# Moving GpSimd's row scatters and value copies behind the weighted sums in a fused attention and mixture-of-experts kernel

## The chip, the cores and the metric

The program runs on one core of a Trainium2 chip. The metric is the time of one execution in microseconds (us), the median of three runs. The core's engines work side by side, each on its own list of instructions, and meet at semaphores: PE (TensorE, matrix multiplication; PEld is its loading of weights), ACT (ScalarE), DVE (VectorE), POOL (GpSimd) and SP (SyncE, which here only issues DMAs).

## The reference, cut to what matters

The input has 8 batches of 512 rows of 128 values. A layer of causal attention with 16 heads of 8 values is followed by a layer that sends every row to its 2 best of 8 experts:

```python
x = L0_attn_x                       # (8, 512, 128)
x = x + attention(layernorm(x))     # causal softmax, 16 heads of 8
# the second layer, on s * b = 4096 rows of 128
probs = jax.nn.softmax(x_flat @ gate_w.T)
topk_probs, topk_idx = jax.lax.top_k(probs, 2)
hidden = relu(einsum('th,ehf->tef', x_flat, w1) + b1)
all_out = einsum('tef,efh->teh', hidden, w2) + b2
y = sum(gathered_by(topk_idx) * topk_probs)
x = x + y
```

The kernel does not compute all experts for all rows. It sorts the rows by expert in memory and works on blocks of 128 rows of one expert.

## The kernel before, in words

**Two stages.** The attention stage is a loop over 8 batches `b` and, in each, 4 groups of 4 heads `g`: 32 steps `s = 4b + g`. The expert stage then works through blocks of 128 sorted rows. Nothing schedules the kernel: each engine has its own function `step(b, g, ...)`, and the order written there by hand is the order in which its instructions run. An engine that waits holds up everything behind it in its list.

**One attention step.** PE makes the scores of step `s + 2` (`scores`, line 998, in 11 pieces; `psS`), and DVE takes their row maxima (`maxima`, lines 1349 and 1352). PE makes the transposed, shifted scores of step `s` (`probs`, line 1011, 10 pieces numbered `n`; `psT`), and ACT takes their exponentials into `PT` (`exps`, line 811). Between them, early in step `s`, PE multiplies the exponentials of step `s - 1` by the values (`weigh`, line 1035, 32 matmuls into `psO`). Its last matmul raises `pv_done`. ACT waits for that to copy the sums out (`copy_heads`, line 816, `Os`), PE then turns them (`turn_heads`, line 1053), and DVE divides them (`norm`). Right behind its weighted sums PE also transposes the split maxima (line 1045, `psM`), and ACT copies those (line 823, `shiftT`).

**What POOL does in a step.** It zeroes the upper triangle of `PT` in four parts: `mask(s, 0)` once `exps(s, 3)` is done, `mask(s, 1)`, `mask(s, 3)`, `mask(s, 2)` once later exponentials are (line 598). It copies the values of a group that the weighted sums have finished with to `Vs` (`load_v`, line 586, four copies, after `pv_done`). In the first group it makes the third part of K (`third_k`, line 559). It splits the maxima of step `s + 2` into three parts (`split_shift`, lines 609 to 617). And it issues the row scatters.

**The row scatters.** A scatter (`scatter`, line 629) is one indirect DMA that POOL issues: 128 normalised rows of 130 values of `xn2` go to the places in `sorted_x` that `place` names. A batch has 4 tiles of 128 rows and 2 experts per row, so 8 scatters. Those of batch `b - 2` are issued in batch `b`, which needs that batch's `place` (semaphore `placed`, by DVE) and `xn2` (`xn2_ready`, by ACT). There are 64 in all, 48 of them in the attention stage from batch 2 on, two in most steps. One stands at a step's end, behind `split_shift`, and so runs into PE's next step; the other stands behind `load_v`. In the last batch there are up to three in a step.

**The counting step.** In the fourth group of a batch (the third group in the last batch) PE counts the rows of each expert for batch `b - 1`: `count_rows`, lines 1073 to 1079, 11 small matmuls in a row. The last one raises `ranks_ready`. DVE makes the places from that.

The program's own names `Qs`, `Ks`, `Vs`, `Os`, `PT`, `psS`, `psT`, `psO`, `psM` are buffers in SBUF or PSUM; `xn` in the rows stands for `xn2` as well.

Of the kernel before, what the change touches and what calls it, by code (L numbers as in the profile page):

```python
# [17 lines left out]
CH = T // P  # L18
TILES = BATCH * CH
GROUPS = 4  # L20
# [13 lines left out]
E, F, TOPK = 8, 512, 2  # L34
# [45 lines left out]
def late_batch(b):  # L80

    return int(b >= KNOWN)
# [50 lines left out]
def prob_turn(s, n):  # L133

    return (s * NPROB + n) % RING, (s * NPROB + n) // RING
# [7 lines left out]
def layer(nc, x, wq, wk, wv, wo, bo, gate_w, w1, b1, w2, b2, out):  # L143
    with ExitStack() as ctx:
# [6 lines left out]
        def sem(name):  # L151
            return ctx.enter_context(nc.semaphore(name))

        def sems(name, n):
            return [sem(f"{name}{i}") for i in range(n)]
# [138 lines left out]
        v_ready, v_copied = sem("v_ready"), sem("v_copied")  # L294
# [7 lines left out]
        prob_ready, prob_done, masked = sems("prob_ready", RING), sems("prob_done", RING), sem("masked")  # L302
        pv_first, pv_done = sem("pv_first"), sem("pv_done")
# [12 lines left out]
        picks_done, ranks_ready, ranks_kept, placed, routed, exp_done = (  # L316
            sem(n) for n in ("picks_done", "ranks_ready", "ranks_kept", "placed", "routed", "exp_done"))
# [192 lines left out]
        def _(pool):  # L510
            def own_wait():

                pool.sem_inc(pool_turn, 1)
# [41 lines left out]
            def third_k(b):  # L555
                u = b % 2
                pool.wait_ge(k_second, b + 1)
                own_wait()
                pool.tensor_tensor(kparts[:, u, 2, :], krest[:, u, :], kparts[:, u, 1, :], ALU.subtract).then_inc(ksplit_done, 1)

            def add_bias(b):
                pool.wait_ge(xn_ready, b + 1)
                own_wait()
                xs = x_all[:, b * CH:(b + 1) * CH, :]
                pool.tensor_tensor(xs, xs, bo_b[:, :].unsqueeze(1).to_broadcast([P, CH, D]), ALU.add).then_inc(xb_done, 1)
# [17 lines left out]
            def load_v(b, g):  # L583
                own_wait()
                for c in range(CH):
                    last = pool.tensor_copy(Vs[:, g, c, :, 0:HD],
                                            v_all[:, b * CH + c, g * 32:(g + 1) * 32].rearrange("p (h d) -> p h d", d=HD))
                last.then_inc(v_loaded, 1)
# [31 lines left out]
            def scatter(b, number):  # L620

                c, k = number // TOPK, number % TOPK
                pool.wait_ge(placed, b + 1)

                if b == BATCH - 2:
                    pool.wait_ge(xn2_last, c + 1)
                else:
                    pool.wait_ge(xn2_ready, (b if b < BATCH - 2 else b - 1) * CH + c + 1)
                pool.indirect_dma_start(  # L629
                    out=xs_dram, out_offset=bass.IndirectOffsetOnAxis(ap=place[:, b, k, c:c + 1], axis=0),  # L630
                    in_=xn2[:, b * CH + c, :], in_offset=None).then_inc(scattered[late_batch(b)], 16)

            def step(b, g, first, last):
                s = b * GROUPS + g
                if last and g > 0:
                    bank, turn = prob_turn(s, 2)
                    pool.wait_ge(prob_done[bank], turn + 1)
                    scatter(b - 2, 3 * g - 2)

                masks = not (last and g == GROUPS - 1)  # L640
                if masks:
                    mask(s, 0)
                if not (first and g == 0) and not (last and g > 0):

                    pool.wait_ge(pv_done, s)
                    pool.wait_ge(v_copied, b + (g + 3) // GROUPS + 1)
                    load_v(b + (g + 3) // GROUPS, (g + 3) % GROUPS)
                if g == 0 and AHEAD_QKV <= b + 1 < BATCH:
                    third_k(b + 1)


                if b >= 2 and g > 0 and not last:
                    scatter(b - 2, 2 * g - 1)
                if last and 0 < g < 3:
                    scatter(b - 2, 3 * g - 1)
                if b >= 3 and g == 0:
                    scatter(b - 3, CH * TOPK - 1)
                if masks:
                    mask(s, 1)
                    mask(s, 3)  # L660
                    mask(s, 2)
                if not (last and g >= 2):
                    split_shift(s + 2, (g + 2) % GROUPS)
                if g == 1 and b + AHEAD_QKV < BATCH:
                    add_bias(b + AHEAD_QKV)
                if g == 3 and b + AHEAD_QKV < BATCH:
                    score_x(b + AHEAD_QKV)
                if b >= 2 and not (last and g > 0):
                    scatter(b - 2, 2 * g)
                if last and 0 < g < 3:  # L670
                    scatter(b - 2, 3 * g)
                if last and g == 3:
                    scatter(b - 1, 0)

# [1202 lines left out]
```

## Time and profile before

| what | us |
|---|---|
| median of three runs | 506.52 |
| lowest and highest of the three | 505.99, 507.28 |
| span of the profiled execution | 527.7 |
| PE busy in that span | 469.7 |
| DVE busy | 413.1 |
| ACT busy | 358.9 |
| POOL busy | 286.6 |

The profiled execution is one run of the same program with the recording of every instruction switched on. Its span, from the first to the last instruction, is 21.2 us longer than the median of the runs without recording. A line of the timeline gives when an operation begins, how long it takes, its engine, line and tiles, how often it is repeated without a gap, and in brackets how long the engine was idle before it and whose work ended the idle time.

### The profile page before, as it was taken

How to read it: one execution, taken by the hardware profiler on the slowest of the kernel's cores; microseconds unless marked ns; L12 is line 12 of the kernel's file. 1: busy time of each engine (PE TensorE's matmuls, PEld its weight loads, DVE VectorE, ACT ScalarE, POOL GpSimd, SP SyncE). 2: the span in 40 equal slices, each digit the busy share in tenths (PEclk: the TensorE clock that was granted, in tenths of full speed). 3: DMA queues.
4: the chain of work that ended last, by engine and by line, in shares of the span. 5: the costliest groups of instructions: out<-in, count | busy, mean ns of one | idle time of the engine just before them, and what ended most of it. 6: DMA issues, size and time to landing. Idle time of an engine off the chain costs nothing.

```text
span 527.7 us, 14330 instructions
## 1 busy us (share of the span) xinstructions
PE 469.7 (89%) x4121; PEld 328.0 (62%) x4121; DVE 413.1 (78%) x1519; ACT 358.9 (68%) x782; POOL 286.6 (54%) x579
## 2 busy tenths in 40 slices
PE   3788999999999999999999999989788789999981
PEld 1545656556555545546555545459688679999980
DVE  6898878988988888888888897875556555557875
ACT  7576877777867867876866857875456457777750
POOL 5603544535755766657657565725456555545542
PEclk9879999999999999999999999999999899999997
DMA  7434232132233233233333326722222322235653
GB/s 225 134 93 129 56 118 91 56 118 88 67 120 108 70 108 110 76 101 97 102 95 98 106 76 175 209 65 63 56 63 69 85 77 74 71 79 180 182 172 101
DMA packets 49454, 54.92 MB, mean 104 GB/s; under 512 B 6564, under 2 KB 41554, under 8 KB 49377
## 3 DMA queue, kind: packets, MB, share of 16 engines
q1 hardware_dynamic: 44736, 45.18, 29.5%
q0 software_dynamic: 4320, 8.47, 4.7%
q8 instruction: 35, 0.57, 0.5%
q14 instruction: 43, 0.34, 0.2%
q10 hardware_dynamic: 320, 0.36, 0.2%
HBM read 34.96 MB, written 17.90 MB: 100 GB/s over the span
## 4 chain that ended last, share of the span: by engine, by line
PE 50%; DVE 28%; ACT 7%; issue 7%; DMA 4%; another core or an unknown queue 3%; ACTq 1%; SPq 0%; POOL 0%; DVEq 0%; POOLq 0%
PE psO L1035 12%; DVE psS L1349 10%; PE psT L1197 7%; DVE maxs L1352 7%; PE psS L998 7%; PE psM L1208 5%; PE psO L1208 5%; PE psT L1011 3%; PE psS L1197 2%; ACT PT L811 2%; DMA xs_t<-sorted_x 2%; PE psS L1187 2%; DVE maxs L1349 1%; DVE xn L1278 1%
## 5 line engine op out<-in xcount | busy, mean ns | idle before, releaser
L811 ACT ACTIVATE PT<-psT 128x512 f32<-128x512 f32 x320 | 172.5, 594 | 67.6 <-PE psO L1035 45.0
L1349 DVE CUSTOM_DVE_ANT_0 psS<-mask_row,psS 128x512 f32<-128x512 bf16 (+1 forms) x232 | 142.8, 624 | 33.6 <-PE psS L998 29.3
L998 PE MATMUL psS<-Ks,Qs 96*128 96x128 bf16 (+3 forms) x512 | 132.9, 308 | 9.5 <-DVE maxs L1352 7.3
L598 POOL TENSOR_SCALAR_AFFINE_SELECT PT<-PT 128x512 f32<-128x512 f32 x124 | 76.8, 635 | 96.0 <-ACT PT L811 94.8
L1011 PE MATMUL psT<-Qs,Ks 108*128 108x384 bf16 (+3 forms) x512 | 109.9, 299 | 4.2 <-ACT PT L811 3.0
L695 POOL DMA_INDIRECT token_y<-Qs,y_row x71 | 70.8, 997 | 74.6 <-DVE Qs L1750 39.0
L998 PEld LDWEIGHTS psS<-Ks,Qs 96*128 96x128 bf16 x512 | 50.4, 99 | 53.5 <-DVE maxs L1352 26.4
L629 POOL DMA_INDIRECT sorted_x<-xn,place x64 | 64.3, 1005 | 27.6 <-issue 16.5
L1352 DVE TENSOR_REDUCE maxs<-psS 128x2 f32<-128x512 f32 (+3 forms) x120 | 75.7, 669 | 1.8 <-PE psS L1001 1.4
L1035 PE MATMUL psO<-PT,Vs 128*32 128x512 f32 (+3 forms) x1024 | 75.8, 436 | 0.3 <-DVE x_all L1375 0.3
L1011 PEld LDWEIGHTS psT<-Qs,Ks 108*128 108x128 bf16 x512 | 43.5, 97 | 32.8 <-ACT PT L811 12.9
L1197 PE MATMUL psT<-turned,qrest 128*128 128x128 f32 x428 | 61.0, 280 | 1.3 <-ACT qrest L887 0.9
L895 ACT ACTIVATE krest<-psT,turned 128x128 f32<-128x128 f32 x142 | 44.7, 365 | 25.7 <-PE psT L1197 8.1
L1197 PEld LDWEIGHTS psT<-turned,qrest 128*128 128x128 f32 x428 | 54.1, 194 | 2.6 <-issue 2.5
L1035 PEld LDWEIGHTS psO<-PT,Vs 128*32 128x32 f32 x1024 | 28.6, 109 | 40.9 <-issue 27.4
L1001 PE MATMUL psS<-mask_row,identb 128*128 128x128 bf16 x280 | 49.9, 226 | 0.0
L887 ACT ACTIVATE qrest<-w_sb 128x512 f32 x71 | 44.6, 630 | 0.4 <-issue 0.4
L882 ACT ACTIVATE turned<-psS 128x128 f32<-128x128 f32 x71 | 19.7, 278 | 35.5 <-PE psS L1187 17.0
L1208 PE MATMUL psO<-w_sb,krest 128*128 x288 | 40.4, 285 | 3.4 <-ACT krest L895 2.3
L1208 PE MATMUL psM<-w_sb,krest 128*128 x280 | 38.2, 279 | 5.7 <-ACT krest L895 3.1
L1743 DVE TENSOR_SCALAR krest<-psS,turned 128x128 f32<-128x128 f32 x70 | 21.5, 347 | 23.0 <-PE psS L1197 12.1
L1208 PEld LDWEIGHTS psO<-w_sb,krest 128*128 128x128 f32 x288 | 36.6, 199 | 4.5 <-issue 4.4
(260 smaller groups left out, 741.1 us busy)
## 6 DMA issues: line engine op xcount, KB each, us to landing
Qs<-q_parts SPq DMA_DIRECT2D x96, 96.0 KB
Ks<-k_parts SPq DMA_DIRECT2D x95, 96.0 KB
xs_t<-sorted_x SPq DMA_DIRECT2D x71, 65.0 KB
w_sb<-in_L_ffn_w SPq DMA_DIRECT2D x16, 256.0 KB
k_parts<-kparts SPq DMA_DIRECT2D x8, 384.0 KB, 2.6
q_parts<-qparts SPq DMA_DIRECT2D x8, 384.0 KB, 3.6
x_all<-in_L_attn_x SPq DMA_DIRECT2D x8, 256.0 KB, 4.7
v_all<-token_y SPq DMA_DIRECT2D x4, 512.0 KB, 4.4
```

The costliest lines, as they stand in the source:

```text
L598: pool.affine_select(out=square, in_=square, compare_op=ALU.is_ge, fill=0.0, base=0, pattern=[[0, GH], [1, P]], channel_multiplier=-1).the ...
L629: pool.indirect_dma_start(out=xs_dram, out_offset=bass.IndirectOffsetOnAxis(ap=place[:, b, k, c:c + 1], axis=0), in_=xn2[:, b * CH + c, :] ...
L695: pool.indirect_dma_start(out=token_y, out_offset=bass.IndirectOffsetOnAxis(ap=y_row[:, i % (2 * Y_RING):i % (2 * Y_RING) + 1], axis=0), i ...
L811: act.activation(PT[:, n * T:(n + 1) * T], psT[:, bank, :], ACT.Exp).then_inc(prob_done[bank], 1)
L998: last = pe.matmul(psS[:, bank, c0:c0 + n], Qs[0:QK_ROWS, g, h, j * P:n], Ks[0:QK_ROWS, g, h, 0:n], start=True, stop=alone)
L1001: last = pe.matmul(psS[:, bank, c0 + n - P:c0 + n], identb[:, :], mask_qk[:, :], start=False, stop=True)
L1011: last = pe.matmul(psT[:, bank, c0:c0 + T - i * P], Ks[0:ST_ROWS, g, h, i * P:(i + 1) * P], Qs[0:ST_ROWS, g, h, i * P:T], start=True, stop ...
L1035: last = pe.matmul(psO[h * VW:(h + 1) * VW, i * P:T], Vs[:, g, i, h, :], PT[:, c0:c0 + cols], start=(i == KEY_BLOCKS[0]), stop=(i == KEY_B ...
L1197: last = pe.matmul(bank[:, c0:c0 + P], w1_t[:, i % 2, c * P:(c + 1) * P], xsT[:, i % 2, :], start=True, stop=True)
L1208: last = pe.matmul(ps_v[i % 2][:, 0:D], hT[:, i % 2, c * P:(c + 1) * P], w2_sb[:, bass.ds(e, 1), c, :].rearrange("p a d -> p (a d)"), star ...
L1349: dve.tensor_tensor_reduce(src, mask_row[:, (CH - 1 - j) * P:], src, 1.0, NEG, ALU.add, ALU.max, maxs[:, par, j, h:h + 1]).then_inc(scores ...
L1352: dve.tensor_reduce(maxs[:, par, j, h:h + heads], src, AX_X, ALU.max).then_inc(scores_used[bank], 1)
```

## The change

All of it is in POOL's list, and no instruction is added or taken away but waits. `load_v`, with its wait for `pv_done`, goes from behind `mask(s, 0)` to the step's beginning. The scatter that stood at a step's end goes to the next step, behind that wait and those copies, ahead of `mask(s, 0)`. The other scatter stays behind `mask(s, 0)`, where now no copies stand between the two; `third_k` goes ahead of it by the same copies. In the counting step it also waits for `ranks_ready`. In the last batch, where `load_v` is over, the wait for `pv_done` alone opens the step, and the waits for exponentials are placed one by one.

```diff
+            def weigh_over(s):
+                pool.wait_ge(pv_done, s)
+
+            def exps_over(s, n):
+                bank, turn = prob_turn(s, n)
+                pool.wait_ge(prob_done[bank], turn + 1)
...
             def step(b, g, first, last):
                 s = b * GROUPS + g
+                masks = not (last and g == GROUPS - 1)
+                if not (first and g == 0):
+                    weigh_over(s)
+                if not (first and g == 0) and not (last and g > 0):
+                    pool.wait_ge(v_copied, b + (g + 3) // GROUPS + 1)
+                    load_v(b + (g + 3) // GROUPS, (g + 3) % GROUPS)
+                if b >= 2 and g > 0:
+                    scatter(b - 2, 3 * (g - 1) if last else 2 * (g - 1))
+                if b >= 3 and g == 0:
+                    scatter(b - 3, CH * TOPK - 2)
+
                 if last and g > 0:
-                    bank, turn = prob_turn(s, 2)
-                    pool.wait_ge(prob_done[bank], turn + 1)
+                    exps_over(s, 2)
                     scatter(b - 2, 3 * g - 2)
-
-                masks = not (last and g == GROUPS - 1)
                 if masks:
                     mask(s, 0)
-                if not (first and g == 0) and not (last and g > 0):
-
-                    pool.wait_ge(pv_done, s)
-                    pool.wait_ge(v_copied, b + (g + 3) // GROUPS + 1)
-                    load_v(b + (g + 3) // GROUPS, (g + 3) % GROUPS)
                 if g == 0 and AHEAD_QKV <= b + 1 < BATCH:
                     third_k(b + 1)
-
-
+                if b >= 2 and g == (2 if last else 3):
+                    pool.wait_ge(ranks_ready, b)
                 if b >= 2 and g > 0 and not last:
                     scatter(b - 2, 2 * g - 1)
-                if last and 0 < g < 3:
-                    scatter(b - 2, 3 * g - 1)
                 if b >= 3 and g == 0:
                     scatter(b - 3, CH * TOPK - 1)
+                if last and 0 < g < 3:
+                    if g == 1:
+                        exps_over(s, 6)
+                    scatter(b - 2, 3 * g - 1)
+
                 if masks:
                     mask(s, 1)
                     mask(s, 3)
...
-                if b >= 2 and not (last and g > 0):
-                    scatter(b - 2, 2 * g)
-                if last and 0 < g < 3:
-                    scatter(b - 2, 3 * g)
                 if last and g == 3:
                     scatter(b - 1, 0)
```

POOL's list in batch 2, from the end of the second step (L565 adds a bias) into the third. Before:

```order
L565 TENSOR_TENSOR x_all<-x_all,bo_b 128x512 [waits xn_ready]
L629 DMA sorted_x<-xn,place 33920x130 [waits xn2_ready,placed]
L598 AFFINE_SELECT PT<-PT 128x4x128 [waits prob_done1]
L586 COPY Vs<-v_all 128x4x8 [waits pv_done,v_copied]
L586 COPY Vs<-v_all 128x4x8 x3
L629 DMA sorted_x<-xn,place 33920x130 [waits xn2_ready,placed]
```

The same place in the changed kernel:

```order
L565 TENSOR_TENSOR x_all<-x_all,bo_b 128x512 [waits xn_ready]
L586 COPY Vs<-v_all 128x4x8 [waits pv_done,v_copied]
L586 COPY Vs<-v_all 128x4x8 x3
L629 DMA sorted_x<-xn,place 33920x130 [waits xn2_ready,placed]
L598 AFFINE_SELECT PT<-PT 128x4x128 [waits prob_done1]
L629 DMA sorted_x<-xn,place 33920x130 [waits xn2_ready,placed]
```

The first scatter and the four value copies now follow PE's weighted sums, and the mask stands between the two scatters.

POOL's list in the fourth step of batch 2, the counting step, from the last part of `split_shift` (L617) of the step before it. Before:

```order
L617 TENSOR_TENSOR mparts<-mrest,mparts 128x4x4 [waits shift_step]
L629 DMA sorted_x<-xn,place 33920x130 [waits xn2_ready,placed]
L598 AFFINE_SELECT PT<-PT 128x4x128 [waits prob_done2]
L586 COPY Vs<-v_all 128x4x8 [waits pv_done,v_copied]
L586 COPY Vs<-v_all 128x4x8 x3
L629 DMA sorted_x<-xn,place 33920x130 [waits xn2_ready,placed]
L598 AFFINE_SELECT PT<-PT 128x4x128 [waits prob_done0] x2
```

The same place in the changed kernel:

```order
L617 TENSOR_TENSOR mparts<-mrest,mparts 128x4x4 [waits shift_step]
L586 COPY Vs<-v_all 128x4x8 [waits pv_done,v_copied]
L586 COPY Vs<-v_all 128x4x8 x3
L629 DMA sorted_x<-xn,place 33920x130 [waits xn2_ready,placed]
L598 AFFINE_SELECT PT<-PT 128x4x128 [waits prob_done2]
L629 DMA sorted_x<-xn,place 33920x130 [waits xn2_ready,placed,ranks_ready]
L598 AFFINE_SELECT PT<-PT 128x4x128 [waits prob_done0] x2
```

Here the second scatter also has a wait for PE's count, and the masks of later exponentials stand behind it. The lists of the other four engines are unchanged.

## Rows read from the trace of the kernel before

**Rows 1.** The page: the span, and busy time, share and instructions of each engine.
```profile
span 527.7 us, 14330 instructions
...
PE 469.7 (89%) x4121; PEld 328.0 (62%) x4121; DVE 413.1 (78%) x1519; ACT 358.9 (68%) x782; POOL 286.6 (54%) x579
```

**Rows 2.** Who waited for whom, whole span: total us, times, longest us.
```profile
ACT Os L816 <- PE psO L1035: 9.8, 13, 1.0
...
PEld psS L998 <- DVE maxs L1352: 26.4, 58, 0.9
```

**Rows 3.** Timeline of POOL, batch 4, second step: start us, us, operation, idle before.
```profile
208.59 1.00 POOL L629 DMA_INDIRECT sorted_x<-xn,place  x1 [0.49 <-issue]
212.78 0.63 POOL L598 TENSOR_SCALAR_AFFINE_SELECT PT<-PT 128x512 f32<-128x512 f32 x1 [3.19 <-ACT PT L811]
213.36 0.65 POOL L586 COPY Vs<-v_all 128x32 f32<-128x32 f32 x4
214.17 1.00 POOL L629 DMA_INDIRECT sorted_x<-xn,place  x1 [0.16 <-issue]
216.34 1.21 POOL L598 TENSOR_SCALAR_AFFINE_SELECT PT<-PT 128x512 f32<-128x512 f32 x2 [1.17 <-ACT PT L811]
```

**Rows 4.** Timeline of ACT: copies of the weighted sums (L816), one exponential (L811).
```profile
107.57 0.60 ACT L816 ACTIVATE Os<-psO 128x512 f32<-128x512 f32 x1
...
189.12 0.60 ACT L816 ACTIVATE Os<-psO 128x512 f32<-128x512 f32 x1 [0.49 <-PE psO L1035]
...
194.36 1.57 ACT L811 ACTIVATE PT<-psT 128x512 f32<-128x512 f32 x3 [0.24 <-PE psT L1011]
...
199.08 0.60 ACT L816 ACTIVATE Os<-psO 128x512 f32<-128x512 f32 x1
...
210.20 0.60 ACT L816 ACTIVATE Os<-psO 128x512 f32<-128x512 f32 x1 [0.92 <-PE psO L1035]
```

**Rows 5.** Timeline of PE: the 32 matmuls of weighted sums; steps of batches 1, 3, 4.
```profile
85.86 2.36 PE L1035 MATMUL psO<-PT,Vs 128*32 128x512 f32 x32
...
95.53 2.36 PE L1035 MATMUL psO<-PT,Vs 128*32 128x512 f32 x32
...
105.14 2.36 PE L1035 MATMUL psO<-PT,Vs 128*32 128x512 f32 x32
...
114.94 2.36 PE L1035 MATMUL psO<-PT,Vs 128*32 128x512 f32 x32
...
186.35 2.36 PE L1035 MATMUL psO<-PT,Vs 128*32 128x512 f32 x32
...
196.65 2.36 PE L1035 MATMUL psO<-PT,Vs 128*32 128x512 f32 x32
...
207.00 2.36 PE L1035 MATMUL psO<-PT,Vs 128*32 128x512 f32 x32
...
217.28 2.36 PE L1035 MATMUL psO<-PT,Vs 128*32 128x512 f32 x32
```

**Rows 6.** Timeline of PE: turning the copied sums, batches 1 and 4.
```profile
89.35 0.60 PE L1053 MATMUL psO<-identf,Os 128*128 128x128 f32 x4
...
210.85 0.66 PE L1053 MATMUL psO<-identf,Os 128*128 128x128 f32 x4 [0.20 <-ACT Os L816]
```

**Rows 7.** Timeline of DVE: two first maxima after the sums, and one square-root step.
```profile
108.07 0.70 DVE L1349 CUSTOM_DVE_ANT_0 psS<-mask_row,psS 128x512 f32<-128x512 bf16 x1 [1.00 <-PE psS L998]
...
189.90 0.70 DVE L1349 CUSTOM_DVE_ANT_0 psS<-mask_row,psS 128x512 f32<-128x512 bf16 x1 [1.64 <-PE psS L998]
...
202.76 0.89 DVE L1418 SCALAR_TENSOR_TENSOR rstd<-near,guess 128x4 f32<-128x4 f32 x1
```

**Rows 8.** One-microsecond stretches: length, busy us and count by engine, clock, DMA, GB/s.
```profile
199.10:200.10 1.00, 1.00 (x8) 0.55 (x6) 0.53 (x1) 1.00 (x3) 1.00 (x1) 1.00 0.42 147
...
208.60:209.60 1.00, 1.00 (x25) 0.67 (x18) 0.47 (x3) 0.68 (x2) 0.99 (x1) 1.00 0.36 111
...
213.40:214.40 1.00, 1.00 (x15) 0.74 (x12) 0.85 (x4) 1.00 (x4) 0.84 (x6) 1.00 0.00 1
```


## The prediction, made before the changed kernel was run

> **What bounds the kernel now.** I read the page first. In a span of 527.7 us PE is busy for 469.7 and DVE for 413.1, while POOL, the only engine whose list changes, is busy for 286.6 [rows 1]. POOL has time to spare, so the change can only matter through those who wait for POOL, or through what POOL's work does to its neighbours. The table of waits comes next. PE waits for DVE's maxima 58 times, 26.4 us in all, and ACT waits for the end of PE's weighted sums before it copies them, 13 times, 9.8 us in all, 0.75 us each [rows 2]. Then I read POOL's timeline in one step. The scatter at the step's end begins at 208.59 and lasts 1.00; the first mask comes at 212.78 after 3.19 us of idle time, then the value copies (0.65), the second scatter (1.00) and, after 1.17 us idle, the next masks [rows 3]. Between the two scatters POOL mostly waits for ACT.
>
> The thing to see is what stands beside the first scatter. In the second step of batch 4 the weighted sums begin at 207.00 and end at 209.36 [rows 5], in the middle of the scatter of 208.59 to 209.59 [rows 3]. ACT starts its copy at 210.20 [rows 4], 0.84 after that end. In the fourth step of batch 1, where no scatter exists yet, the sums end at 107.50 [rows 5] and the copy starts at 107.57 [rows 4]: 0.07. In the fourth step of batch 3 it is 189.12 against 188.71: 0.41. In the first step of batch 4 the sums end at 199.01 and the copy starts at 199.08, again 0.07, though POOL is in a scatter from then on [rows 4, 5, 8]. So PE's word that the sums are over reaches ACT late when it falls inside a scatter, and on time when it falls ahead of one. That is what the change is about: it puts the first scatter behind that word.
>
> **The change part by part.** *The first scatter leaves the end of the sums.* What the late word costs can be read in three places. PE turns the copied sums 1.13 after their end in batch 1 (89.35 against 88.22) and 1.49 after it in batch 4 (210.85 against 209.36) [rows 5, 6]: 0.36 lost on PE. DVE takes its first maximum behind the sums 0.57 after their end in batch 1 (108.07) and 1.19 after it in batch 3 (189.90 against 188.71) [rows 5, 7]: 0.62 lost on DVE. And whole fourth steps take 9.80 in batch 1 (105.14 to 114.94) and 10.30 in batch 3 (186.35 to 196.65): 0.50 [rows 5]. Second steps take 9.67 and 10.28 [rows 5], 0.61 apart, of which I give the scatter only PE's 0.36, since ACT has normalisations to do there from batch 2 on. Five second steps (batches 2 to 6) by 0.36 make 1.8, five fourth steps by 0.50 make 2.5, and the three waits that are left of the 13, in the last batch, by 0.36 make 1.1: together 5.4 us of the profiled span. The bounds are 0 and 13 by 0.62, or 8.1.
>
> *What the first scatter meets in its new place.* After the sums' end come the copies (0.65), a gap of 0.16 and the scatter (1.00) [rows 3]: about 1.8 us, with the signal some 2. The first mask starts at 212.78, 3.4 after the end of the sums. So it hides with 1.4 to spare, and POOL's idle time of 3.19 is the cover; if that were gone, each step would lose up to 1.8. I take 0.
>
> *The second scatter and the copies.* With the copies out of the way the second scatter starts 0.65 earlier, at some 213.5 instead of 214.17, and the masks behind it, which wait for ACT in any case (1.17 idle), lose nothing [rows 3]. The same goes for the third part of K in the first steps: 0.65 earlier on POOL, with nobody waiting. It can change what it blocks, though: in a first step an operation of DVE on 4 values per partition takes 0.89 [rows 7]. At most it frees or costs 0.65 in each of five steps, 3.3 either way. I take 0, since the maxima's waits of PE stand elsewhere in most steps.
>
> *The wait for the count.* Six counting steps now hold POOL until PE has counted. Behind the waiting scatter stand three masks and the splitting of the maxima, and PE waits for the latter. On PE's own list the count stands ahead of the scores' exponentials that the next mask needs, so POOL's 1.17 of idle time covers the scatter's 1.00 plus 0.16 [rows 3]: barely. The bounds are 0 and six by 1.16, or 7.0. I take 0, because the mask can't start before ACT's exponential, which comes later than the count. The gain there is bounded by ACT's wait of 0.24 at 194.36, just behind a count [rows 4], and is already in the 0.50.
>
> *The last batch.* The wait for an exponential ahead of the third scatter of the second step may push the masks back by a scatter, 1.0 us once at most; I take 0.
>
> The sum on the profiled execution is 527.7 - 5.4 = 522.3 us.
>
> **How this stands to the timed runs.** Their median is 506.5, 21.2 us under the profiled span, though a span has nothing around it and a timed run does. So there are at least 21 us of delay in the profiled execution that the timed runs don't have, and the question is whether the 5.4 are among them. One more row bears on that. In the microsecond in which the word was late PE had 25 matmuls and 18 weight loads, 43 instructions; in the one in which the scatter did no harm it had 8 and 6 [rows 8]. Both stretches have nearly the same DMA share (0.36 and 0.42), so the number of PE's instructions tells them apart and the traffic doesn't. A path that carries a record for each instruction would be short exactly there. The sums' matmuls themselves take 2.36 us in every step, with and without a scatter [rows 5]: no engine works more slowly, only a message comes late.
>
> The Trainium skill's page "NOTIFIC — the notification-queue block", section "7.1 Overflow: three behaviours, one of which stalls the engine", says that the block that writes such records holds its producers back when its inner queues fill, rather than lose one. By that rule the late word is made by the recording, and the timed runs would gain 0 where the rows of the profiled execution give 5.4. No row here shows such a queue.
>
> **The rivals.**
> 1. *The late word belongs to the recording* (chance 0.50). For it: the 21.2 us, and the count of 43 against 14. Against it: ACT and DVE are really late in the trace, and an indirect DMA could as well hold a real message up. Then the scatters and copies move inside idle time, and the time stays: 506.5 less some tenths for masks that wait no longer, 506.2, between 505.0 and 508.0.
> 2. *The late word is real* (0.37). For it: the chain from the sums over ACT's copy back to PE, and steps that are longer by 0.50. Then the timed runs gain what the span gains, 5.4: 501.1. Part of it may come back at the second scatter, which moves into a denser stretch, so 501 to 504.5.
> 3. *The second scatter does what the first did* (0.10), the one that ends slower. It starts 0.65 earlier, and the microsecond from 213.40 has 15 matmuls and 12 loads, 27 instructions, between the 14 that did no harm and the 43 that did [rows 8]. If 27 is enough, each of the first three steps of batches 2 to 6 has a late message: 15 by 0.50 is 7.5, less the 5.4 is 2.1 slower, 508.6. It decides itself by whether ACT's waits for the transposed scores grow at that place.
> 4. *Anything else that costs over 1.5 us*, the masks of the counting steps before all (0.03): six by 0.5 or so, 509.5.
>
> That the moved wait isn't what holds the scatter is no rival of its own: the list of POOL shows it ahead of the copies and the scatter.
>
> **How the numbers follow.** The likeliest single case is the first, 506.2. Within 0.3% (1.5 us, about what a measurement of this kernel can tell from no change) lies nearly all of it and nothing of the others: 0.50. Faster is the second, 0.37. Slower are the third and fourth, 0.13. The range has to take in the second case's most likely part: from 501.0 it leaves out 0.05 below; up to 508.4 it leaves out about 0.10. The likeliest case's own range is 505.0 to 508.0.
>
> **What would show it.** Right for the first scatter: in the profile after, ACT's copies start 0.07 after the sums' end in all steps, the 13 waits of 9.8 us are gone, and fourth steps of batches 2 to 5 take 9.8. The span then falls by about 5 while the median stays (first rival) or falls as well (second). Wrong for the second scatter: new waits of ACT for the transposed scores right behind the first mask. Wrong for the count: the masks of the fourth steps start later after the count than now, and PE waits for the split maxima. The prediction itself is wrong if the median falls with the span, since then the 21.2 us lie in other delays than these.

## The result: slower by half a per cent

The changed kernel takes 509.97 us (median of four, 508.38 to 510.50) where the kernel before takes 506.90 (505.99 to 507.62) beside it. The ratio is 1.0051, with a 95% interval of 1.0030 to 1.0073: slower by about 2.6 us by the ratio (3.1 us between the medians). The forecast was 506.2, the range ended at 508.4.

The page of the changed kernel, the span and the first line on the engines:

```profile
span 506.6 us, 14330 instructions
...
PE 461.6 (91%) x4121; PEld 327.8 (65%) x4121; DVE 412.7 (81%) x1519; ACT 360.3 (71%) x782; POOL 287.2 (57%) x579
```

This span is 21.1 us shorter than that of [rows 1], PE's busy time 8.1, and yet the timed runs are longer. Neither the spans nor their difference can be taken for what the change did; why is the first finding of the experiments.

Three readings answer to the rows of before. The wait of ACT for the weighted sums, 13 times and 9.8 us in [rows 2], is down to one of 0.2 us (table of waits, same columns as there):

```profile
PEld psS L1009 <- DVE maxs L1363: 25.4, 56, 0.7
...
PEld psS L1009 <- DVE maxs L1360: 7.0, 12, 2.5
...
ACT Os L827 <- PE psO L1046: 0.2, 1, 0.2
```

(Lines behind POOL's step stand 11 further down than before: L1035 is now L1046, L816 is L827, L1349 is L1360, L1278 is L1289.) The second line has a longest wait of 2.5 us, longer than any of PE for DVE's maxima in the trace of before. It shows in the starts of the weighted sums (timeline of PE), to be held against [rows 5]:

```profile
185.45 2.36 PE L1046 MATMUL psO<-PT,Vs 128*32 128x512 f32 x32
195.25 2.36 PE L1046 MATMUL psO<-PT,Vs 128*32 128x512 f32 x32
208.99 2.36 PE L1046 MATMUL psO<-PT,Vs 128*32 128x512 f32 x32
218.77 2.36 PE L1046 MATMUL psO<-PT,Vs 128*32 128x512 f32 x32
```

The steps take 9.80, 13.74 and 9.78. The fourth step of batch 3 is as fast as that of batch 1 (9.80), and the second step of batch 4 takes 9.78 where [rows 5] have 10.28. But the step from 195.25, the first of batch 4, takes 3.39 more than the 10.35 of [rows 5] (196.65 to 207.00). What happened in it, on POOL and on DVE (two timelines of the same stretch):

```profile
199.01 1.09 POOL L629 DMA_INDIRECT sorted_x<-xn,place  x1 [0.53 <-issue]
200.13 0.64 POOL L598 TENSOR_SCALAR_AFFINE_SELECT PT<-PT 128x512 f32<-128x512 f32 x1
200.73 1.15 POOL L559 TENSOR_TENSOR kparts<-krest,kparts 128x512 bf16<-128x512 f32 x1
202.05 0.98 POOL L629 DMA_INDIRECT sorted_x<-xn,place  x1 [0.17 <-issue]
```

```profile
198.86 0.34 DVE L1289 TENSOR_SCALAR xn<-x_all,mean,rstd 128x128 f32<-128x128 f32 x1
...
199.66 2.30 DVE L1289 TENSOR_SCALAR xn<-x_all,mean,rstd 128x128 f32<-128x128 f32 x1
199.92 2.50 DVE L1360 CUSTOM_DVE_ANT_0 psS<-mask_row,psS 128x384 f32<-128x384 bf16 x1
```

L1289 normalises 128 values per partition from SBUF to SBUF. It takes 0.34 at 198.86 and 2.30 at 199.66, and the maximum queued behind it ends 1.95 late as well. POOL's L559 ends at 201.88, L1289 at 201.97, and the maximum then at 202.42. PE waits for that maximum, and then its clock falls (two-microsecond stretches; length, busy us and count by engine, then PEclk, DMA share, GB/s):

```profile
200.00:202.00 2.00, 0.34 (x3) 0.06 (x1) 2.00 (x2) 1.34 (x3) 1.86 (x3) 1.00 0.28 58
202.00:204.00 2.00, 1.46 (x13) 1.46 (x14) 1.97 (x11) 0.00 (x0) 0.98 (x1) 0.75 0.59 194
204.00:206.00 2.00, 2.00 (x12) 1.60 (x11) 0.99 (x3) 0.60 (x1) 0.00 (x0) 0.50 0.15 45
```

PE stands still for 2.20 us, from 200.34 to 202.54. After that its granted clock is 0.50, the lower level (1.2 GHz), until 206.4. The 1.95 of the hold-up become 3.39.

### The profile page after: what moved, and what is told of

It is laid out like the page before. It is cut to its first block, busy times and chain, and to the rows that moved or that the text cites. A ratio compares the mean times of both kernels' runs of the same rounds, so it can differ in the third digit from the quotient of the medians.

```text
span 506.6 us, 14330 instructions
## 1 busy us (share of the span) xinstructions
PE 461.6 (91%) x4121; PEld 327.8 (65%) x4121; DVE 412.7 (81%) x1519; ACT 360.3 (71%) x782; POOL 287.2 (57%) x579
## 4 chain that ended last, share of the span: by engine, by line
PE 57%; DVE 26%; issue 5%; DMA 5%; ACT 4%; POOL 2%; SPq 1%; ACTq 0%; DVEq 0%; POOLq 0%
PE psO L1046 13%; DVE psS L1360 9%; PE psS L1009 8%; PE psT L1208 7%; DVE maxs L1363 7%; PE psO L1219 5%; PE psM L1219 5%; PE psT L1022 5%; PE psS L1208 2%; DMA xs_t<-sorted_x 2%; PE psM L1056 1%; ACT PT L822 1%; PE psS L1198 1%; PE psS L1012 1%; DVE maxs L1360 1%
## 5 line engine op out<-in xcount | busy, mean ns | idle before, releaser
L1360 DVE CUSTOM_DVE_ANT_0 psS<-mask_row,psS 128x512 f32<-128x512 bf16 (+1 forms) x232 | 144.7, 632 | 29.8 <-PE psS L1009 29.6
L1046 PE MATMUL psO<-PT,Vs 128*32 128x512 f32 (+3 forms) x1024 | 75.8, 436 | 0.0
L1208 PE MATMUL psT<-turned,qrest 128*128 128x128 f32 x428 | 59.8, 276 | 0.0
L1046 PEld LDWEIGHTS psO<-PT,Vs 128*32 128x32 f32 x1024 | 28.4, 109 | 40.7 <-issue 28.2
L1219 PE MATMUL psO<-w_sb,krest 128*128 x288 | 38.8, 278 | 0.6 <-issue 0.6
L1219 PEld LDWEIGHTS psM<-w_sb,krest 128*128 128x128 f32 x280 | 34.0, 192 | 3.9 <-issue 3.6
```

The source lines that it names most:

```text
L1046: last = pe.matmul(psO[h * VW:(h + 1) * VW, i * P:T], Vs[:, g, i, h, :], PT[:, c0:c0 + cols], start=(i == KEY_BLOCKS[0]), stop=(i == KEY_B ...
L1208: last = pe.matmul(bank[:, c0:c0 + P], w1_t[:, i % 2, c * P:(c + 1) * P], xsT[:, i % 2, :], start=True, stop=True)
L1219: last = pe.matmul(ps_v[i % 2][:, 0:D], hT[:, i % 2, c * P:(c + 1) * P], w2_sb[:, bass.ds(e, 1), c, :].rearrange("p a d -> p (a d)"), star ...
L1360: dve.tensor_tensor_reduce(src, mask_row[:, (CH - 1 - j) * P:], src, 1.0, NEG, ALU.add, ALU.max, maxs[:, par, j, h:h + 1]).then_inc(scores ...
```

## The measure used below

The first 48 to 50 us and the expert stage are not steady from one profile of a kernel to the next: the two of the changed kernel differ by 1.4 and 1.6 us, and the expert stage of the three called two_behind_t, _u and _q below by up to 10 us. The stretch from PE's first weighted sums to the start of its last differs by 0.15 and 0.5 us in the same profiles, so it is the measure of the runs: "attention" below. The changed kernel has 296.97 in the profile above and 297.12 in the next one:

```profile
48.30:345.27 296.97, 283.29 (x2664) 167.19 (x2663) 260.61 (x959) 220.55 (x440) 181.45 (x425) 0.99 0.35 103
```

One thing has to be known of the sessions in which kernels ran together. In three of them (the result's, and those of the next two groups) the kernel before takes 506.8 to 507.8 us, in the other three 532.7 to 535.1. I call them short and long sessions. What sets them apart isn't known; chip 7 had one of each kind. Ratios are taken inside a session; attention is compared between sessions of one kind too.

| kernel | session | attention | stall in batch 4 | ratio to before (95%) |
|---|---|---|---|---|
| before_again | short | 294.33 | no | 0.9995 (0.9969 to 1.0022) |
| changed (result; after_again) | short | 296.97; 297.12 | yes | 1.0051; 1.0027 (0.9999 to 1.0055) |
| no_count_wait | short | 295.66 | yes | 1.0034 (0.9998 to 1.0070) |
| k_behind | short | 297.97 | shorter, and three others | 1.0079 (1.0039 to 1.0119) |
| first_old | short | 293.71 | no | 0.9975 (0.9940 to 1.0009) |
| only_first | short | 297.76 | yes | 1.0040 (1.0001 to 1.0079) |
| two_behind | short | 293.66 | no | one run, 505.41 us |
| shifted | short | 293.66 | no | one run, 506.22 us |
| rows of before | - | 300.13 | no | |
| before_shifted | long | 300.12 | no | 1.0011 (0.9976 to 1.0046) |
| after_t (changed) | long | 296.23 | yes | 0.9964 (0.9931 to 0.9996) |
| shifted_t | long | 294.22 | no | 0.9911 (0.9878 to 0.9944) |
| two_behind_t, _u, _q | long | 294.76, 294.36, 294.25 | no | 0.9938, 0.9914, 0.9914 |
| scatter_only, _q | long | 294.58, 294.54 | no | 0.9899, 0.9941 |
| copies_only | long | 301.62 | no | one run, 536.59 us |

## First group: is it the stall, and what were the 21 us?

*The kernel before once more.*

> The kernel before, unchanged, for a second profiled execution. The first one had a span of 527.7 us, 21.2 over the median of the times; the profiled execution of the changed kernel had 506.6, 3.4 under its median. Theory A: the 21 us belong to that one execution. Then this profile has a span near 505, attention still shows the late copies behind the first scatters (13 waits, 9.8 us), and the stretch behind 350 us is about 156 long instead of 178. Theory B: recording always lengthens the kernel before by some 21 us and not the changed one. Then the span is near 527 again. Time 506.5 in both.

```profile
span 506.4 us, 14330 instructions
...
ACT Os L816 <- PE psO L1035: 2.4, 8, 0.5
```

The span is 506.4, so the 21 us belong to the execution shown ahead of the prediction, as theory A has it, and not to recording. The execution profiled here is also one of the timed ones: its own time is 508.19, among others from 505.23 to 509.17. Theory A was wrong on one point: here ACT waits for the sums 8 times and 2.4 us in all, not 13 times and 9.8. Of 18 sums that end inside a scatter 11 have their copy 0.07 behind the end, as where there is no scatter. The latest copy, in the second step of batch 4, comes 0.46 behind the end instead of 0.84, and yet that scatter has the same 25 matmuls and 18 weight loads beside it as in [rows 8]. So neither a scatter around the sums' end nor PE's count of instructions is enough for a word as late as in the rows. Attention takes 294.33, and fourth steps take 9.91 to 9.94 instead of the 10.30 of [rows 5].

*The changed kernel once more.*

> The changed kernel, unchanged. Its first profile shows one step of 13.74 us instead of 10.35: DVE's L1360 took 2.50 instead of 0.55 while POOL was in the mask L598 and third_k L559, PE stood 2.36 us and its clock then fell to half. Theory A (this stall is what made it slower): it comes back at the same place or in another first step of a batch, once or more, and the time is some 3.4 us per stall above an execution without one; time 509.5 to 510.5. Theory B (an accident of that execution): no such stall in this profile, a span of about 503, and the time at 510 must come from elsewhere.

The stall is there in the same step (L1289 takes 2.31 at 201.11, the step 13.75). It is no accident. Attention is 2.79 us longer than in before_again, as much as the 2.6 us of the result. The time missed theory A's 509.5 to 510.5, though: the median is 508.29, the ratio 1.0027, with an interval that just takes in 1.

*third_k behind the second scatter.*

```diff
-                if g == 0 and AHEAD_QKV <= b + 1 < BATCH:
-                    third_k(b + 1)
...
                 if b >= 3 and g == 0:
                     scatter(b - 3, CH * TOPK - 1)
+                if g == 0 and AHEAD_QKV <= b + 1 < BATCH:
+                    third_k(b + 1)
```

> The changed kernel with third_k behind the second scatter instead of between the first mask and that scatter, so that no two operations of POOL on 512 columns follow each other there. Theory A (mask and third_k back to back hold DVE for 2 us, worth 3.4 us once): the 2.50 us operation is gone, all first steps of batches 2 to 5 take 10.3 to 10.4, and the time is 506.5, 3.4 under the changed kernel. Theory B (the loss is spread or lies elsewhere): the time stays at 509.5 to 510.5.

Theory A's time failed (511.29, ratio 1.0079), and the trace tells more for it. In batch 4 L1289 is held for the mask alone and takes 1.19. But the first steps of batches 3, 5 and 6 now have a hold-up at the second scatter, since third_k follows it at once. The longest (POOL, then DVE):

```profile
282.74 0.97 POOL L629 DMA_INDIRECT sorted_x<-xn,place  x1 [0.16 <-issue]
283.74 1.17 POOL L559 TENSOR_TENSOR kparts<-krest,kparts 128x512 bf16<-128x512 f32 x1
284.85 1.80 POOL L598 TENSOR_SCALAR_AFFINE_SELECT PT<-PT 128x512 f32<-128x512 f32 x3
```

```profile
283.45 3.22 DVE L1435 SCALAR_TENSOR_TENSOR offset<-mv,rstd 128x4 f32<-128x4 f32 x1
```

An operation on 4 values per partition, 0.15 us elsewhere, began 0.71 into a scatter and ended at 286.67. POOL's last mask ended at 286.65. It was held for one third_k and three masks, as many as POOL had in a row without a gap. As in batch 4 of the changed kernel, an operation of DVE from SBUF to SBUF that began 0.6 to 0.7 us into a scatter, with POOL's next operation directly behind, waited until POOL's whole run was over.

The Trainium skill, page "SBUF — State Buffer", section "Who interferes with whom", says that DVE, in some of its modes or with two inputs in SBUF, and GpSimd share a port pair as an exclusive lock, and that the one that comes second is blocked until the other has finished. The trace agrees that POOL's work blocks DVE's; it doesn't show a port. On the length it differs: by the page the wait would end with one operation, here it lasted over four. Where no scatter is ahead the length agrees too. In batch 1 of every trace an operation on 4 values begins 0.03 behind the start of L565 and takes 1.27, as long as L565 alone; in the changed kernel it doesn't wait for the value copies that follow L565 at once (L1407 at 97.99, L565 at 97.96).

*No wait for the count.*

```diff
-                if b >= 2 and g == (2 if last else 3):
-                    pool.wait_ge(ranks_ready, b)
```

> The changed kernel without POOL's wait for the count in the counting steps (six waits less, nothing else). Theory A (that wait is covered, as the prediction took it): same time as the changed kernel, within 0.7 us, and fourth steps at 9.80. Theory B (the wait costs): up to six by 0.5 us, so 3 us faster than the changed kernel, about 507.

The stall stands, but the clock stayed up (granted 1.00 from 204 to 206), and so the step takes 12.30 instead of 13.75. Without the stall's part attention would be 295.66 - 1.95 = 293.71; for the changed kernel it is 297.12 - 3.40 = 293.72. In these profiles the wait for the count costs nothing, and in the times nothing that can be told from it (507.84 against 508.29).

## Second group: where the loss sits, and on what it hangs

*POOL's list in the first steps as before, elsewhere as changed.* The first scatter of a first step goes back to the end of the step ahead of it, the copies go behind the mask.

```diff
-                if b >= 3 and g == 0:
-                    scatter(b - 3, CH * TOPK - 2)
                 if masks:
                     mask(s, 0)
+                if g == 0 and not first:
+                    weigh_over(s)
+                    pool.wait_ge(v_copied, b + 1)
+                    load_v(b, 3)
...
+                if b >= 2 and g == 3 and not last:
+                    scatter(b - 2, CH * TOPK - 2)
```

> The changed kernel, but POOL's list in the first step of each batch as before: the first scatter at the end of the step ahead of it, then the first mask, the value copies, third_k, the second scatter. Theory A (the stall in the first step is the whole loss, and what the other steps gain is some 0.6 us): no operation of DVE above 1.3 us in attention, all first steps of batches 2 to 5 at 10.35, attention from the first weighted sums to the last 293.6 to 294.0 us (before_again 294.3, after_again 297.1), time 506.2, or 0.1% under before and 2.5 to 3.5 under the changed kernel. Theory B (the loss is spread over the other steps): time 508.5 to 510.

*The counterpart: only the first steps as changed.* The same lines the other way round, in the kernel before.

> The counterpart: the kernel before, with only the first steps of the batches as changed (value copies, first scatter, first mask, third_k, second scatter). Theory A (the first step holds the loss): a stall of 1.9 us or more on DVE in batch 4 as in the changed kernel, that step 12.3 to 13.8 instead of 10.35, time 2 to 3.4 us above before, about 509.5. Theory B (the loss is elsewhere): no such stall, time 506.5.

Both come out as theory A has it. first_old has no stall, attention 293.71 and 506.32 us against 507.83; only_first has the same operation (L1283 there) at 2.31 in batch 4, that step at 13.92 and 509.68 us. The loss sits in the first step of batch 4, and the other steps gain 294.33 - 293.71 = 0.62 us together. Most of it is the fourth steps: three at 9.80 instead of 9.91 to 9.94, one at 9.89 instead of 9.92, and 9.03 instead of 9.09 in batch 6. The times alone don't show this gain: the interval of 0.9975 takes in 1.

*Both scatters behind third_k.*

```diff
-                if b >= 3 and g == 0:
-                    scatter(b - 3, CH * TOPK - 2)
...
                 if b >= 3 and g == 0:
+                    scatter(b - 3, CH * TOPK - 2)
                     scatter(b - 3, CH * TOPK - 1)
```

> The changed kernel with both scatters of the first step behind third_k: value copies, first mask, third_k, then the two scatters. Mask and third_k still follow each other without a gap, but no scatter runs into the mask. Theory A (what holds DVE's L1289 is the end of a scatter with POOL's next operation right behind it): no stall ahead of the mask, first steps 10.35, unless the second scatter now runs into the next masks. Theory B (mask and third_k back to back are enough): an operation of DVE of 1.8 to 2.5 us at the first mask of one or more batches.

Theory A: attention 293.66. Mask and third_k stand without a gap here too, and L1289 runs freely 0.21 ahead of them (DVE, then POOL):

```profile
200.22 0.34 DVE L1289 TENSOR_SCALAR xn<-x_all,mean,rstd 128x128 f32<-128x128 f32 x1
```

```profile
200.43 0.64 POOL L598 TENSOR_SCALAR_AFFINE_SELECT PT<-PT 128x512 f32<-128x512 f32 x1 [1.37 <-ACT PT L822]
201.03 1.16 POOL L559 TENSOR_TENSOR kparts<-krest,kparts 128x512 bf16<-128x512 f32 x1
```

So the pair alone doesn't make the stall where L1289 is already under way, and no operation of DVE is held for both. Nor is the scatter enough. In only_first an operation of the same kind begins 0.73 into a scatter that has 0.97 of idle time behind it, and is not held:

```profile
323.23 0.16 DVE L1429 SCALAR_TENSOR_TENSOR offset<-mv,rstd 128x4 f32<-128x4 f32 x1
```

```profile
322.50 0.97 POOL L629 DMA_INDIRECT sorted_x<-xn,place  x1 [0.16 <-issue]
324.44 1.80 POOL L598 TENSOR_SCALAR_AFFINE_SELECT PT<-PT 128x512 f32<-128x512 f32 x3 [0.97 <-ACT PT L816]
```

All 19 traces taken together bear this out for the attention stretch. 16 operations of DVE were held to the end of a run of POOL behind a scatter, over up to four operations. Each began 0.62 to 0.72 into the scatter, with POOL's next operation at most 0.03 behind it. With no scatter ahead no hold-up covered more than one whole operation that POOL began after it; the longest of that kind, L1404 at 333.29 in the changed kernel, begins within one mask, ends with the next and takes 0.79 instead of 0.23. A gap of 0.15 was enough to be let through: in the changed kernel an operation of L1463 began 0.63 into the scatter of 300.41 and took its usual 0.18. And the kind of operation counts. A reduction from SBUF to SBUF (L1549 at 339.48) began 0.70 into a scatter with three masks directly behind and took 0.32, as elsewhere; ten other traces have the same.

*Why batch 4 only?* In the changed kernel the first scatter of batch 3's first step begins 0.22 behind the copies and ends 0.13 ahead of the mask. In batch 4 it begins 0.53 behind them and runs into the mask:

```profile
158.96 1.03 POOL L629 DMA_INDIRECT sorted_x<-xn,place  x1 [0.22 <-issue]
160.12 0.63 POOL L598 TENSOR_SCALAR_AFFINE_SELECT PT<-PT 128x512 f32<-128x512 f32 x1
```

The edit of shifted computes nothing; it puts 24 waits that are already met ahead of the loop and so moves all later instructions back in POOL's list (the trace counts 12 instructions more).

```diff
             third_k(0)
             pool.wait_ge(const_step, 10)
+            for _ in range(24):
+                pool.wait_ge(const_step, 10)
```

> The changed kernel with 24 waits that are already met in POOL's list, ahead of the attention loop: nothing that computes changes, only the places of all later instructions in POOL's list. In three profiles the first scatter of batch 4's first step begins 0.53 us behind the value copies, in the other batches 0.22. Theory A (the 0.31 us belongs to a place in the list, as the fetch of instructions would make it): the late scatter, and with it the stall, is in another step or in none, and the attention stage is up to 3.4 us shorter. Theory B (it belongs to batch 4): the 0.53 and the stall stay.

```profile
200.27 1.03 POOL L629 DMA_INDIRECT sorted_x<-xn,place  x1 [0.22 <-issue]
201.43 0.63 POOL L598 TENSOR_SCALAR_AFFINE_SELECT PT<-PT 128x512 f32<-128x512 f32 x1
...
298.90 1.01 POOL L629 DMA_INDIRECT sorted_x<-xn,place  x1 [0.45 <-issue]
```

Theory A. In batch 4 the scatter is on time, a late one now stands at 298.90 where it does no harm, the stall is gone, and attention is 293.66. The 0.31 us hang on the place in POOL's list, not on the batch. Whether the fetching of instructions makes them no run shows.

## Third group: the same in long sessions

The next three sessions were long ones, and that settled what the 21 us were.

> The kernel of two_behind, timed. Its profile had attention at 293.66 us from the first weighted sums to the last, against 294.33 in before_again and 297.12 in after_again. Theory A (attention decides): 0.65 us under before, 0.1%, so a ratio of 0.998 to 1.000, and 3 us under the changed kernel. Theory B (something outside attention also pays for the new order): a ratio above 1.002.

> The kernel of shifted, timed: the changed kernel with 24 waits that are already met, ahead of POOL's attention loop. Theory A (the changed kernel is slow through one stall that hangs on the place of an instruction in POOL's list): ratio to before 0.998 to 1.000. Theory B (the profile was a lucky one): ratio 1.003 to 1.006, as the changed kernel.

> The changed kernel once more, on the same chip as the two ahead of it. Theory A: a ratio of 1.005 to 1.007 to before, attention 297.0 in the profile, with the stall of 1.95 us on DVE in batch 4. Theory B: stall absent, ratio 1.000.

> The control: the kernel before with the same 24 waits. Theory A (the shift helps only by taking the stall away, which the kernel before doesn't have): same time as before, ratio 0.999 to 1.001, attention 294.2 to 294.5 us. Theory B (the shift itself gains elsewhere): ratio 0.996 or less.

before_shifted is the kernel before with the 24 waits. Its trace is that of [rows 2] over again:

```profile
ACT Os L818 <- PE psO L1037: 9.9, 13, 1.0
...
PEld psO L1055 <- ACT Os L818: 6.0, 10, 1.1
```

13 waits, 9.9 us, attention 300.12 (300.13 in the trace ahead of the prediction). The timed runs of before beside it have a median of 532.70, and the profiled execution's own time, 531.21, lies among those of its kernel (528.28 to 535.75). So the profile is like the timed runs here as well. The rows of before match such a session, while the 506.5 beside them match a short one. The control itself does what theory A says: the shift alone moves nothing (1.0011).

The expectations for the other three missed their ratios, all on the same side: in a long session the change gains. The changed kernel is faster than before, 0.9964 (0.9931 to 0.9996), although it has its stall (12.27 for that step, the clock stayed up); without it (shifted_t) the ratio is 0.9911. In attention the step from 300.12 to 294.22 is 5.90 us; the prediction's sum for the first scatter was 5.4. These gains are in the timed runs, so the late word is real there.

*Which part of the move gains?* scatter_only is the changed kernel with the value copies back behind the mask; copies_only is the kernel before with the copies alone moved ahead.

```diff
-                if not (first and g == 0) and not (last and g > 0):
-                    pool.wait_ge(v_copied, b + (g + 3) // GROUPS + 1)
-                    load_v(b + (g + 3) // GROUPS, (g + 3) % GROUPS)
...
                 if masks:
                     mask(s, 0)
+                if not (first and g == 0) and not (last and g > 0):
+                    pool.wait_ge(v_copied, b + (g + 3) // GROUPS + 1)
+                    load_v(b + (g + 3) // GROUPS, (g + 3) % GROUPS)
```

> The changed kernel with the value copies put back behind the first mask, so that of the move only the first scatter's is left. It now starts some 0.65 us earlier and ends ahead of the first mask. Theory A (the scatter's place gains, the copies' place only pushes the scatter into the mask): no stall in batch 4, attention from the first weighted sums to the last at 293.7 us on a chip like the first two, 294.3 on one like the third. Theory B (the copies' place gains): attention as before, 294.3 and 300.1. On the third chip's kind the time would be 1% under before by A, on the others 0.1%.

> The kernel before with only the value copies put at the beginning of the step; all scatters as before. Theory A: attention as before, 294.3 us on a chip like the first two, 300.1 on one like the third, with the late copies behind the first scatters as before. Theory B (the copies' place gains): 293.7 or 294.3.

> The kernel of two_behind a second time, timed, in the hope of a chip like the first two. Theory A (attention decides, and the late words are made only where they were seen): ratio 0.998 to 1.000 on a chip like the first two (attention 293.7 against 294.3), 0.990 to 0.994 on one like the third (294.8 against 300.1). Theory B: the gain is the same on all chips, 0.994.

```profile
48.17:342.75 294.58, 282.07 (x2664) 165.97 (x2664) 261.22 (x958) 221.07 (x440) 180.71 (x425) 1.00 0.34 104
48.92:350.54 301.62, 286.62 (x2665) 164.82 (x2664) 258.84 (x958) 221.26 (x440) 181.56 (x425) 1.00 0.33 102
```

The first line is scatter_only, the second copies_only. The scatter's place gains all of it, the copies' place gains nothing. copies_only still has 14 waits of ACT for the sums, 10.0 us, and takes 1.5 us longer than before, in one profile: the first steps of batches 3 to 5 take 10.91 to 10.94 instead of 10.35. What makes them longer wasn't followed. With the copies behind the mask the scatter also ends well ahead of the mask, and batch 4 has no stall. Its ratio is 0.9899 (0.9864 to 0.9933).

> The kernel of scatter_only once more. In a session like the last two (before at 530 to 535) the expectation is that of its first run: 0.990. In a session like the first ones (before at 506 to 508): attention 293.7 against 294.3, ratio 0.998 to 1.000, if the late words are all that it gains from; 0.994 or less, if it gains from something that all sessions have.

> The kernel of two_behind beside it: attention within 0.3 us of scatter_only's in either kind of session, and the same ratio within the intervals.

Again a long session. The ratios are 0.9941 (0.9912 to 0.9969) and 0.9914 (0.9885 to 0.9944), with attention 0.3 apart. (In long sessions every kernel with the changed last batch has one more hold-up of the same kind there, 2.1 us on the conversion of the last places behind a scatter and three masks; attention of 294.2 to 294.8 instead of 293.7 holds its price.) Both beat the kernel before and, by their attention, the changed one. Whether their 0.6 us show in a short session's times stays open: there is the single 505.41 of two_behind against a median of 507.83, and first_old's 0.9975 with an interval that takes in 1.

## Why the prediction was wrong

Two steps failed. What put the time outside the range is the first scatter's new place and third_k behind it, both taken at 0: together they cost 3.4 us in the first step of batch 4. The other is how the profile stands to the timed runs; it put the likeliest case on a reason that the runs don't bear out.

**The late word is there, and what removes it.** Right for its removal. The 13 waits are down to one of 0.2 us and fourth steps take 9.80, as written. Wrong as a rule: that the word is late whenever it falls inside a scatter held in the rows and in before_shifted, but in before_again only for 7 sums of 18. The sum of 5.4 us for the profiled session's kind was near too: 5.90 (shifted_t against before_shifted) and 5.54 (scatter_only).

**How this stands to the timed runs.** This step failed. I read the 21.2 us between span and median as the cost of recording. They were the difference between two kinds of session. The profile of before_again has a span of 506.4 with all recording on. The count of 43 instructions against 14 in [rows 8] doesn't tell the two apart either, since before_again has the same 43 and half the delay, and no run shows a queue of records that holds an engine: timed runs of long sessions gain from the change. Without the stall the likeliest case would have come near, by luck, for the wrong reason: in a short session the late words are few, 8 waits and 2.4 us, and their removal is worth 0.6 us of attention.

**The first scatter's new place, taken at 0.** This step failed: in one first step it cost 3.4 us, together with third_k. The cover of 3.19 us idle time came from a second step [rows 3]. In a first step the mask starts earlier: in the execution of [rows 7] at 201.27, 2.26 after the end of the sums at 199.01, while copies, gap and scatter were put at some 2. So 0.3 us were to spare by these rows, not 1.4; in batch 3 of the changed kernel it was 0.13. One scatter that began 0.31 late used them up, and ran into the mask.

**third_k, 0 between -3.3 and 3.3.** The row that told it was [rows 7]: an operation of DVE on 4 values took 0.89 beside POOL's third_k. I priced it at the 0.65 by which third_k moved. What counts is not how far it moves but what it now stands against: mask and third_k in one run behind a scatter, 1.8 us for which DVE can be held, and PE behind DVE. With the clock's fall this made 3.4, just outside the bound, and it came once instead of five times.

**The wait for the count** cost nothing, as taken (293.71 against 293.72). **The second scatter** did not do what the first did (rival 3): the second to fourth steps of batches 2 to 5 take 9.78 to 9.82, where the rival had 0.5 more in each. **The last batch**: its steps take 8.35, 7.33 and 5.26, within 0.1 of before_again's.

**The rivals.** Rival 1 gave the size without the stall, rival 2 was right for long sessions, and neither of those on the slower side named DVE. A slower rival should have been the blocking of [rows 7] worked out for its worst place.

## What to carry to other kernels

Work out a cover for each kind of step, not for the best shown one, and ask of each POOL operation that is moved with what it will form a run: an SBUF-to-SBUF operation of DVE can be held for the whole run behind a scatter. Leave a gap on POOL (0.15 us was enough here), or put scatters last, where DVE feeds PE. And before a difference between a profile and the times is explained, see the same kernel profiled beside its times.

## What was unexpected in the hardware

- Behind a scatter DVE's hold-up lasts as long as POOL's run: 1.19 us in all (one mask), 1.51 (third_k), 2.30 (mask and third_k), 3.22 (third_k and three masks), where the operation takes 0.34, 0.29 or 0.15 elsewhere. A reduction at the same place was not held (0.32).
- 24 waits that were already met, ahead of the loop, took a stall of 3.4 us away by moving a 0.31 us delay to another scatter.
- Behind 2.2 us of standing still PE lost its clock in after, after_again and only_first (the step 13.74, 13.75 and 13.92), and not in no_count_wait and after_t (12.30 and 12.27). What decides it stays open.
- The same program takes 507 us in one session and 533 in another. Attention has 5.8 of the difference, in late words behind scatters; most of the rest is in the expert stage (163 us behind the start of the last sums in before_again, 181 in before_shifted). What makes a word late in one kind of session and not in the other stays open.
